# Attention block on one Trainium2 core: the next unit's values projected one double step later, and behind the products with the values instead of ahead of them

## The reference, cut to what matters

```python
h = layernorm(x)
q = einsum('bsd,dhk->bshk', h, Wq) + bq      # k and v likewise
attn = softmax(einsum('bqhd,bkhd->bhqk', q / 8, k))
out = einsum('bhqk,bkhd->bqhd', attn, v)
x = x + layernorm(einsum('bqhd,hdm->bqm', out, Wo) + bo)
x = x + layernorm(ffn(layernorm(x)))         # U1, V1, gelu, U2, V2
```

## Time and profile before

| | |
|---|---|
| median of 3 runs | 2379.12 us |
| lowest and highest | 2377.48 and 2380.11 us |
| the profiled execution | 2382.51 us |
| its span, first to last instruction | 2380.7 us |
| TensorE busy with matmuls | 2341.8 us, 98% |
| GpSimd, VectorE, ScalarE busy | 89%, 87%, 58% |
| mean granted TensorE clock | 0.991 of full |
| data moved | 62.54 MB, 26 GB/s |

### The profile page before, as it was taken

One profiled execution on the slowest core, in us unless ns is written; L12 is line 12 of the kernel. 1 busy time (PEld: TensorE's weight loads), 2 busy tenths in 40 slices (PEclk: granted clock), 3 DMA queues, 4 the chain that ended last, 5 costly groups with the idle time before them and its releaser, 6 DMA issues.

```text
span 2380.7 us, 43479 instructions
## 1 busy us (share of the span) xinstructions
PE 2341.8 (98%) x15632; PEld 1181.5 (50%) x15632; DVE 2066.7 (87%) x3166; ACT 1380.4 (58%) x1672; POOL 2112.9 (89%) x1210
## 2 busy tenths in 40 slices
PE   6999999999999999999999999999999999999998
PEld 3445455545555455454554545554554545544454
DVE  7888888888888888888888888888888888889977
ACT  6655556565555655555555655656556565655545
POOL 6888989989889988989989898988989898899986
PEclk8999999999999999999999999999999999999999
DMA  2000001000000000100000000100000000110101
GB/s 59 28 14 28 28 15 32 28 15 28 28 19 28 28 16 26 33 22 20 28 22 25 28 28 15 32 28 15 28 28 19 28 28 15 35 32 19 37 28 36
DMA packets 63895, 62.54 MB, mean 26 GB/s; under 512 B 29796, under 2 KB 47588, under 8 KB 63684
## 3 DMA queue, kind: packets, MB, share of 16 engines
q1 hardware_dynamic: 62820, 59.51, 8.5%
q10 hardware_dynamic: 864, 0.26, 0.0%
HBM read 56.88 MB, written 2.61 MB: 25 GB/s over the span
## 4 chain that ended last, share of the span: by engine, by line
PE 95%; DVE 2%; POOL 1%; issue 1%; ACT 0%; DMA 0%; POOLq 0%; DVEq 0%; ACTq 0%
PE o_ps L455 38%; PE spare_ps L410 14%; PE score_ps L434 10%; PE score_ps L440 10%; PE score_ps L437 10%; PE spare_ps L396 3%; PE spare_ps L500 3%; PE spare_ps L387 3%; PE spare_ps L378 3%; PE spare_ps L467 1%; DVE max_part L895 1%; POOL total L1177 1%; DVE ln_stats L867 0%; PE spare_ps L480 0%; PE score_ps L548 0%
## 5 line engine op out<-in xcount | busy, mean ns | idle before, releaser
L1177 POOL TENSOR_TENSOR total<-total,probs 128x832 f32<-128x832 f32 (+1 forms) x896 | 1761.5, 1966 | 225.1 <-ACT probs L722 151.9
L895 DVE TENSOR_REDUCE max_part<-spare_ps 128x1 f32<-128x512 f32 x2027 | 1303.3, 685 | 266.0 <-PE spare_ps L410 251.8
L722 ACT ACTIVATE probs<-score_ps 128x1024 f32<-128x1024 f32 x1024 | 993.0, 1022 | 815.0 <-PE score_ps L440 814.9
L455 PE MATMUL o_ps<-probs,v_sb 128*64 128x512 f32 x4096 | 980.8, 599 | 0.0
L455 PEld LDWEIGHTS o_ps<-probs,v_sb 128*64 128x64 f32 x4096 | 266.4, 136 | 451.4 <-issue 280.6
L410 PE MATMUL spare_ps<-k_hi,q_hi 64*128 64x512 f32 x2027 | 462.6, 450 | 8.9 <-DVE max_part L895 4.4
L410 PEld LDWEIGHTS spare_ps<-k_hi,q_hi 64*128 64x128 f32 x2027 | 194.0, 184 | 429.6 <-issue 228.6
L434 PE MATMUL score_ps<-q_hi,kd_hi 64*128 64x512 f32 x2048 | 407.1, 393 | 0.0
L440 PE MATMUL score_ps<-q_hi,kd_lo 64*128 64x512 f32 x2048 | 405.1, 391 | 0.0
L437 PE MATMUL score_ps<-q_lo,kd_hi 64*128 64x512 f32 x2048 | 404.4, 390 | 0.0
L938 DVE TENSOR_REDUCE part_sum<-probs 128x192 f32<-128x768 f32 (+1 forms) x255 | 392.7, 1540 | 0.7 <-ACT probs L722 0.7
(11 more groups left out here) (142 smaller groups left out, 1167.1 us busy)
## 6 DMA issues: line engine op xcount, KB each, us to landing
m_all<-m_scratch SPq DMA_DIRECT2D x64, 512.0 KB, 4.4
denom<-denom_scratch SPq DMA_DIRECT2D x122, 128.0 KB, 2.9
m_scratch<-neg_rows SPq DMA_DIRECT2D x256, 1.0 KB
y_acc<-in_L_attn_x SPq DMA_DIRECT2D x8, 256.0 KB, 6.1
key_f<-in_L_attn_x SPq DMA_DIRECT2D x8, 256.0 KB, 2.8
block_out<-probs SPq DMA_DIRECT2D x8, 256.0 KB, 2.3
denom_col<-denom SPq DMA_DIRECT2D x61, 4.0 KB
denom_scratch<-denom_col SPq DMA_DIRECT2D x61, 4.0 KB, 1.4
```

Of the source, the lines that this page charges most:

```text
L455: last = nc.tensor.matmul(o_ps[half(h), :], v_sb[:, b, kt, half(h)], probs[:, st % RING, h, :], start=(kt == 0), stop=(kt == T - 1))
L722: nc.scalar.activation(probs[:, st % RING], score_ps[st % 2][:], ACT.Exp, scale=SCALE).then_inc(s["exp_done"], 1)
L895: nc.vector.reduce_max(max_part[:, G % 2, h, qt, kc:kc + 1], bank[max_bank(n, h)], AX.X).then_inc(s["max_done"], 1)
L1177: nc.gpsimd.tensor_tensor(others(total[:, G % 2], G), so_far, others(probs[:, st % RING], G), ALU.add).then_inc(s["sum_done"], 1)
```

## The change

The values of the next unit are projected at d = 6, not d = 5. In every double step that projects values, also the three of `OWN_V_AT`, TensorE issues the projection behind the values' products, not ahead of them. The places of ScalarE's copy in its queue follow `values_at`: it moves from d = 5 to d = 6 and keeps its place there, behind the exponentials and ahead of keys and queries. `spare_banks` is not edited; it follows `values_at` too, with the values' bank ahead of the queries' in a double step that has both.

```diff
-V_AT = {(0, 5): (0, 4), (1, 5): (4, 4), (2, 5): (8, 4), (3, 5): (12, 4)}
+V_AT = {(0, 6): (0, 4), (1, 6): (4, 4), (2, 6): (8, 4), (3, 6): (12, 4)}
...
-FIRST_V_AT = {(0, 5): (0, 4), (1, 5): (4, 4), (2, 5): (8, 4), (3, 5): (12, 4)}
+FIRST_V_AT = {(0, 6): (0, 4), (1, 6): (4, 4), (2, 6): (8, 4), (3, 6): (12, 4)}
...
                     me.project_k(*keys_at(u, c, d))
-                if values_at(u, c, d):
-                    me.project_v(*values_at(u, c, d))
                 if d == Q_AT and G + 2 < CHUNKS:
                     me.project_q(G + 2)
...
                 if n:
                     me.values(2 * n - 2)
                     me.values(2 * n - 1)
+                if values_at(u, c, d):
+                    me.project_v(*values_at(u, c, d))
                 if d == L_AT and 0 < G <= CHUNKS - COLUMN_CHUNKS:
                     me.denominators(G - 1)
```

## The result

| | before | changed |
|---|---|---|
| median of 6 runs | 2379.53 us | 2389.16 us |
| lowest and highest | 2377.48 and 2381.35 | 2388.59 and 2392.85 |
| span of the profiled execution | 2380.7 | 2387.4 |

The changed kernel is slower by a factor of 1.0043 (95% interval 1.0033 to 1.0053), 9.6 us.

A forecast was written before the change was run, and what follows sets the result against it. TensorE, busy 98%, was taken to bound the kernel. Quarters +4.7 and unit 0 +5.2 made +9.9 us, 2392.4 on the profiled execution, 2389.0 us as median; range 2382 less 1 to 2393.3 plus 1.2.

The forecast's parts named there:

- The projection: On TensorE, 0.87 us leaves d = 5 and enters d = 6 in 60 places, with no drain behind the products: net 0.
- The wait at d = 7 and the seed: TensorE's 0.10 us wait appears at d = 6; the seed lets d = 7 return only 0.02: +0.08 per quarter, +4.7 us.
- my one row: The timeline stretch at d = 7, 2.30 us and not 2.20, from which a wait of 0.10 us was read.
- Behind the copy nothing else is queued at d = 6, except in unit 0: On ScalarE's queue, the later values' copy was claimed to delay no other work outside unit 0: price 0.
- Unit 0: Waits by banks and by ScalarE's queue at n = 2 and n = 6: +5.2 us, bounds 3 and 6.5.
- n = 2 to 4: Unit 0: queries wait +1.0, next maxima pair +0.9, second pair of n = 3 +0.4, bias product +0.3: 2.6 us.
- n = 6 and what follows: Unit 0: projection, values' copy, keys' copies and VectorE delay the next maxima pair by 2.5, with d = 6's 0.1: +2.6 us.
- the gap that I foresaw: Near 83 us in unit 0, a stretch of 2.5 us with no matmul, ended by VectorE's L921.
- The sum: Whole kernel: 4.7 us from the quarters plus 5.2 from unit 0, +9.9 us, forecast 2389.0 us.
- only moves: Rival, chance 0.2: d = 7 gains its whole 0.10 to 0.12 us, d = 6 pays it; only unit 0 costs, 2384.3.
- the drain: Rival, chance 0.1: the array drains between products and projection, as ahead of the denominator sums: +8.7 us, 2397.7.
- not slower: Rival, chance 0.1: late maxima at d = 6 do not hold TensorE and d = 7 gains in full: -1.3 us, 2377.8.

The follow-up runs named there:

- e3: Kernel before, with units 1 to 15 projecting values behind the products but still at d = 5: 2380.41 us, ratio 0.9994 to before.
- e6: Change in units 1 to 15 alone, with VectorE's share of the probabilities' sums cut from 192 to 176 columns: 2378.60 us, ratio 0.9997 to before.
- e7: Change in units 1 to 15 alone, with ScalarE's seed over one head, not both, except in the first quarter (times only): 2379.64 us, ratio 0.9998 to before.
- e8: Kernel before, with ScalarE's seed over one head, not both, in every quarter but the first (times only): 2378.53 us, ratio 0.9994 to before.
- e10: Kernel before, with VectorE's share of the probabilities' sums cut from 192 to 176 columns: 2380.02 us, ratio 0.9996 to before.
- e1: Changed kernel with unit 0 projecting values as before, so the change is in units 1 to 15 alone: 2383.14 us, ratio 1.0008 to before.
- e5: Changed kernel with ScalarE's copy of the values moved behind all its other work of the double step: 2385.18 us, ratio 1.0020 to before.
- e9: Kernel before, with units 1 to 15 projecting values at d = 7 ahead of the products, VectorE's share 176 columns: 2377.84 us, ratio 0.9989 to before.
- e11: Kernel before, with units 1 to 15 projecting values at d = 7 behind the products, VectorE's share 176 columns: 2374.90 us, ratio 0.9983 to before.
- e4: Kernel before, with units 1 to 15 projecting values at d = 6 but still ahead of the products: 2389.21 us, ratio 1.0025 to before.
- e2: Changed kernel with units 1 to 15 as before, so the change is in unit 0 alone: 2389.49 us, ratio 1.0029 to before.

## Why the prediction was right, point by point

**The projection: right.** Its cost moved from d = 5 to d = 6 and nothing drained (e3).

**The wait at d = 7 and the seed: right, a little too dear.** I had +0.10 at d = 6, and 0.02 back from d = 7, as the seed holds d = 0. All of it is in the traces, and e6, e7, e8 and e10 show each cause. The size: +3.5 us in 57 quarters is 0.06 each and not 0.08. On average d = 6 pays 0.09, d = 7 gives 0.12 and d = 0 takes 0.10, so the 0.02 back was right; another 0.01 us a quarter comes back over d = 1 to 4, which I had at nothing. d = 7 had waited for 0.10 to 0.15 us, and my one row was one of the shorter waits.

**"Behind the copy nothing else is queued at d = 6, except in unit 0": wrong.** At n = 470 and 478 the feed-forward's normalisation stands behind the copy. I had checked the queue of a usual quarter and not the lists of the last units. It made n = 471 and 479 longer by 0.8 us each, of which 0.5 comes back at n = 480 (e1, e5). The rest of the 2.3 us of that stage is n = 488, and it comes back at n = 496.

**Unit 0: the chains right, the sum too small by 1.0.** n = 2 to 4 cost 2.2 us, where I had 2.6. n = 6 and what follows cost 4.0 where I had 2.6. The missing term is the clock: the gap that I foresaw is followed by 3.3 us at half the clock.

**The sum: right partly by luck.** Against my 9.9 us the quarters cost 1.2 less, unit 0 1.0 more and the stage from n = 465 to 489, which I had at nothing, 2.3 more; n = 496 then gave 2.8 back, 1.7 of it because a stretch at half the clock is missing there. I foresaw neither of the last two. What is left is 9.1 us in the profiled executions and 9.6 by the medians. That the medians came within 0.2 us of the forecast is luck; that they moved up by most of 10 us is not. **The rivals:** "only moves" is refuted by e7 and e8 and by the seed's distance to the scores in every quarter, the drain by e3, "not slower" by the trace of d = 6.

## What to carry to other kernels

When a wait of a repeated step goes, look for the next event that is late by the same amount, at an engine other than the one that waited: here a seed on ScalarE stood 0.1 us behind VectorE's maxima, and taking either away alone won little. When work on an in-order engine comes to depend on a later producer, list everything behind it in every stage of the kernel, the first and the last too, and not only in the usual one. And a rare stretch can cost as much as a repeated one: the first of 16 units paid 6.2 us of about 9. Last, when a stage of a trace differs where nothing was changed, find the double step that differs before putting it down to the clock.

## What was not expected of the hardware

- A gap of 2.3 us on TensorE in mid-kernel was followed by 3.3 to 3.4 us at half the granted clock, in both kernels that had it, and it cost 1.6 us more: n = 7 took 5.51 us in the changed kernel and 3.91 before. The length of the gap alone doesn't tell: the gap of 1.81 us at n = 496 of before was followed by 3.4 us at half the clock, that of 1.78 at n = 496 of e5 and that of 2.55 at n = 488 of the changed kernel were not. What decides stays open. The row of the last one, at full clock (columns as above):

```profile
2226.00:2232.00 6.00, 3.48 (x20) 1.60 (x22) 4.99 (x14) 2.33 (x4) 5.86 (x4) 1.00 0.00 0
```

- A projection ahead of the products lengthens a late second pair by 0.06 to 0.09 us against the same work behind them (averages of d = 7 in e9 and e11, and of d = 6 in e4 and the changed kernel).
- At n = 488 of the changed kernel two VectorE operations (L1035 and L1040) took 1.33 and 1.71 us, where before each took 0.68. They waited for GpSimd:

```profile
2222.31 1.96 POOL L1177 TENSOR_TENSOR total<-total,probs 128x832 f32<-128x832 f32 x1
2223.48 1.33 DVE L1035 TENSOR_TENSOR xn<-y_acc,ln_rstd 128x512 f32<-128x512 f32 x1
```

GpSimd's addition was running when L1035 started. It ended at 2224.26, and L1035 at 2224.81, 0.55 us later. In all nine kernels where these two operations took longer than 0.68 us, each ended 0.55 us behind the end of a GpSimd operation that was running when it started. Before, L1035 and the addition started within 0.02 us of each other; L1035 took its 0.68 and the addition 2.54 in place of 1.96. So what n = 488 costs hangs on a few hundredths of a microsecond between the two. The two operations take 2.48 and 1.66 us in e4, which has no late copies at n = 471 and 479, 1.92 and 1.17 in e11, and 0.68 each in e2, e3, e5 and e8.
